# The mask product leaves the scores of two graph attentions, and VectorE adds the mask in place of ScalarE's copy

## The reference, cut to what matters

```
h = layernorm(x) @ W
e = leaky_relu(h @ a1 [:, None] + h @ a2 [None, :], 0.2)
e = where(adj > 0, e, -1e9)            # 128 x 128 for each graph
out = softmax(e) @ h
x = x + elu(out)
```

## Time and profile before

| | |
|---|---|
| median of 3 runs | 587.17 us (584.67 to 588.05) |
| the profiled execution | 585.35 us, its span 583.6 us |
| PE | 544.2 us busy, 93% of the span |
| DVE | 447.8 us, 77% |
| ACT | 418.4 us, 72% |
| POOL | 232.1 us, 40% |
| chain that ended last | PE 78%, issue 6%, DVE 5%, POOL 5%, ACT 4% |

### The profile page before, as it was taken

One profiled execution on the slowest core, in us unless ns is written; L12 is line 12 of the kernel. 1 busy time (PEld: TensorE's weight loads), 2 busy tenths in 40 slices (PEclk: granted clock), 3 DMA queues, 4 the chain that ended last, 5 costly groups with the idle time before them and its releaser, 6 DMA issues.

```text
span 583.6 us, 15065 instructions
## 1 busy us (share of the span) xinstructions
PE 544.2 (93%) x3792; PEld 452.0 (77%) x3825; DVE 447.8 (77%) x1652; ACT 418.4 (72%) x1102; POOL 232.1 (40%) x449
## 2 busy tenths in 40 slices
PE   6678999999999999999999999999977999999993
PEld 5556678777787878778777787767756799999993
DVE  3766979889898898988989888776555377777777
ACT  1355667878878788787887878877643578888883
POOL 6222214442434424334243342331322036666665
PEclk8999999999999999999999999999999799999998
DMA  8504325052250522505235051230320377777732
GB/s 202 121 14 151 95 69 165 6 160 83 82 163 1 162 79 84 159 4 162 71 91 163 0 163 35 76 110 9 102 72 2 120 223 242 247 236 218 221 119 72
DMA packets 78834, 66.46 MB, mean 114 GB/s; under 512 B 9916, under 2 KB 64460, under 8 KB 78796
## 3 DMA queue, kind: packets, MB, share of 16 engines
q1 hardware_dynamic: 65562, 60.60, 34.0%
q10 hardware_dynamic: 13234, 5.42, 3.4%
HBM read 61.57 MB, written 4.42 MB: 113 GB/s over the span
## 4 chain that ended last, share of the span: by engine, by line
PE 78%; issue 6%; DVE 5%; POOL 5%; ACT 4%; ACTq 1%; DVEq 0%; POOLq 0%
PE bank L1496 14%; PE bank L1483 13%; PE wide L206 5%; PE bank L1728 5%; PE bank L1738 4%; PE wide L1728 4%; PE wide L239 4%; PE wide L1738 4%; PE bank L1475 3%; PE bank L1476 3%; PE bank L1477 3%; PE wide L231 2%; PE wide L199 2%; PE wide L1524 2%; PE wide L220 2%
## 5 line engine op out<-in xcount | busy, mean ns | idle before, releaser
L1496 PE MATMUL bank<-w,h2w 128*128 128x128 f32 x768 | 104.2, 279 | 1.8 <-DVE h2w L1080 1.8
L1496 PEld LDWEIGHTS bank<-w,h2w 128*128 128x128 f32 x768 | 94.8, 192 | 6.9 <-DVE h2w L1080 3.0
L1483 PE MATMUL bank<-h,w 128*128 128x512 f32 x192 | 98.8, 596 | 0.3 <-ACT h L821 0.3
L816 ACT ACTIVATE h<-bank,b 128x512 f32<-128x512 f32 x96 | 66.3, 690 | 41.7 <-PE bank L1483 41.5
L821 ACT ACTIVATE h<-bank,b 128x512 f32<-128x512 f32 x96 | 66.0, 688 | 12.9 <-PE bank L1477 12.7
L1080 DVE TENSOR_TENSOR h2w<-h,wide_w 128x512 f32<-128x512 f32 x96 | 64.8, 676 | 8.2 <-ACT h L816 8.0
L1475 PE MATMUL bank<-xnTh,w1h 128*128 128x512 f32 x96 | 66.9, 697 | 0.0
L100 POOL TENSOR_TENSOR route_var_eps<-route_mean_var,eps 128x4 f32<-128x4 f32 x16 | 10.4, 651 | 115.2 <-DVE route_mean_var L93 115.1
L100 POOL TENSOR_TENSOR at_var_eps<-at_mean_var,eps 128x4 f32<-128x4 f32 x32 | 12.9, 403 | 94.0 <-DVE at_mean_var L93 94.0
L268 ACT ACTIVATE at_pr<-at_lk,at_nm 128x128 f32<-128x128 f32 x128 | 41.3, 414 | 3.6 <-DVE at_nm L303 3.6
L206 PE MATMUL wide<-at_wc,at_xT 128*128 128x130 f32 x256 | 36.0, 286 | 5.1 <-ACT at_xT L247 5.1
(11 more groups left out here) (264 smaller groups left out, 1364.0 us busy)
## 6 DMA issues: line engine op xcount, KB each, us to landing
wide_w<-w_scratch SPq DMA_DIRECT2D x96, 256.0 KB, 4.5
mask<-in_L_ffn_W SPq DMA_DIRECT2D x124, 128.0 KB, 2.4
x<-in_x SPq DMA_DIRECT2D x16, 256.0 KB, 5.1
adj_in<-in_adj SPq DMA_DIRECT2D x16, 256.0 KB, 5.8
wide_w<-bmix_scratch SPq DMA_DIRECT2D x16, 256.0 KB, 3.6
xin<-in_x SPq DMA_DIRECT2D x15, 256.0 KB, 5.6
out<-at_pr ACTq DMA_DIRECT2D x8, 256.0 KB, 3.1
out<-at_prT ACTq DMA_DIRECT2D x7, 256.0 KB, 2.8
```

Of the source, the lines that this page charges most:

```text
L816: a.activation(h2[:, e % 2, :], b_h2[:, :], ACT.Relu, bias=b2[:, e:e + 1]).then_inc(h2_ready, 1)
L1483: pe.matmul(b_h2[:, :], w2[:, e, :], h1[:, e % 2, :], start=True, stop=True).then_inc(l2_done, 1)
L1496: last = pe.matmul(b_out[:, s], h2w[:, e % 2, s], w3[:, e, :], start=False, stop=(e == E0 - 1), skip_group_check=True)
```

## The change

The product L219 is taken out in both attentions, and L220 starts the accumulation instead. `attn_act_z`, ScalarE's copy of the scores, is taken out. `attn_dve_max` begins with a new VectorE addition, which reads the scores in PSUM and the mask in SBUF and writes `lk`; the two old VectorE instructions follow it. TensorE no longer waits for the mask, VectorE waits for TensorE's scores. Nothing else moves.

```
-def attn_pe_scores(st, pe, identb, mask, spread, g):
+def attn_pe_scores(st, pe, spread, g):
     pe.wait_ge(st["rows_ready"], g + 1)
-    pe.matmul(st["bank"][:, :], identb[:, :], mask[:, cols(g)], start=True, stop=False, skip_group_check=True)
-    pe.matmul(st["bank"][:, :], st["rows"][:, :], spread[:, 0, :, :].rearrange("p t d -> p (t d)"), start=False,
+    pe.matmul(st["bank"][:, :], st["rows"][:, :], spread[:, 0, :, :].rearrange("p t d -> p (t d)"), start=True,
               stop=False, skip_group_check=True)
...
-def attn_act_z(st, a, g):
-    a.wait_ge(st["z_done"], g + 1)
-    need(a, st["x_ready"], g)
-    a.activation(st["lk"][:, :], st["bank"][:, :], ACT.Copy).then_inc(st["z_ready"], 1)
...
-def attn_dve_max(st, v, g):
+def attn_dve_max(st, v, mask, const_ready, mask_ready, g):
+
+    settle(v, const_ready)
+    v.wait_ge(st["z_done"], g + 1)
+    v.wait_ge(mask_ready, g + 1)
+    need(v, st["x_ready"], g)
+    v.tensor_tensor(st["lk"][:, :], st["bank"][:, :], mask[:, cols(g)], ALU.add).then_inc(st["z_ready"], 1)
     v.wait_ge(st["z_ready"], g + 1)
     v.scalar_tensor_tensor(st["lk"][:, :], st["lk"][:, :], SLOPE, st["lk"][:, :], ALU.mult, ALU.max)\
         .then_inc(st["lk_ready"], 1)
...
                 if attn0:
-                    attn_act_z(at0, a, i + 2)
...
-                if attn1:
-                    attn_act_z(at1, a, i - 1)
...
                 if attn0:
-                    pe.wait_ge(mask_ready, i + 3)
-                    attn_pe_scores(at0, pe, identb, mask, spread, i + 2)
+                    attn_pe_scores(at0, pe, spread, i + 2)
```

More of the change, by code:

```diff
@@ L877, in body @@
                     attn_act_elu(at1, a, i - 2)
-                if attn0:
-                    attn_act_z(at0, a, i + 2)
                 def route_relu(g):
@@ L1225, in body @@
                 if attn0:
-                    attn_dve_max(at0, v, i + 2)
+                    attn_dve_max(at0, v, mask, const_ready, mask_ready, i + 2)
                 if live("norm0", i0) and i0 != -LEAD["route"]:
@@ L1242, in body @@
                     if i0 == N:
-                        attn_dve_max(at1, v, N - 1)
+                        attn_dve_max(at1, v, mask, const_ready, mask_ready, N - 1)
                     if i0 >= N:
@@ L1267, in body @@
                 if attn1 and i0 != N:
-                    attn_dve_max(at1, v, i - 1)
+                    attn_dve_max(at1, v, mask, const_ready, mask_ready, i - 1)
                 if live("route", i0, 1) and i0 != -LEAD["route"]:
@@ L1636, in body @@
                 if attn1:
-                    attn_pe_scores(at1, pe, identb, mask, spread, i - 1)
+                    attn_pe_scores(at1, pe, spread, i - 1)
                 if run:
```

## The result

The changed kernel takes 603.69 us, the median of 6 runs (601.97 to 606.23), and the kernel before 587.49 us in 6 runs beside it (584.67 to 590.44). The ratio is 1.0278, with an interval from 1.024 to 1.0317. The forecast was 594.8 us. The direction is right and the loss is twice the forecast: 16.2 us where 7.6 were worked out.

The account below looks back on a forecast made before the run. TensorE's own stream and a mixed ring over ScalarE, VectorE and layer 3 were taken to share the bound. Losses of 3.0 + 3.0 + 1.4 + 0.7, less 0.3 and 0.2, gave +7.6 us: 594.8 us, range 586.5 to 599.

Parts of the forecast that it names:

- The ring through `at1`: L1477, ScalarE, `p_sum`, VectorE's list, layer 3, next L1477: `at1`'s addition inside it makes the next round 0.60 us late.
- The bare hand-overs: Layer 3's weight loads for e = 0 and e = 5 follow VectorE's multiplication by 0.06 us every round.
- the sum: Rounds 2 to 14 lose 3.0 + 3.0 + 1.4 us; with the last group and small savings, net +7.6 us.
- TensorE's idle time behind `h2w`: Sign: TensorE idles about 0.35 (e = 3), 0.35 (e = 5) and 0.5 (e = 0) us a round.
- it costs nothing: `at0`'s addition, ahead of L299, takes its time out of VectorE's 1.75 us wait at `p_sum`; uncovered, 0.72 a round.
- The cover: VectorE's wait at `p_sum` for ScalarE's `pe`, 1.75 us a round, taken as hiding `at0`'s addition.
- the last group: Round 16, where L299 follows a norm that waited for GpSimd and little else runs: 0.7 us lost.
- TensorE's stream deciding: Rival: TensorE's stream sets the time, so removing its products saves 7.0 us, giving 580.2 us; chance 0.12.
- The two cancelling: Rival: ScalarE's freed 0.59 brings `p_sum` forward about as much as the addition delays e = 0; 587 us, chance 0.13.
- VectorE becomes the bound: Rival: additions cost 0.93 each and nearly use up the 1.8 us cover; about +10.5 us, 597.7 us, chance 0.08.
- The rule that was weighed: Skill's rule putting each VectorE addition at 0.61 instead of 0.72, making the result 1.8 us lower; rows 4 preferred.

Follow-up runs that it names:

- e1: Kernel before with the change made in the second attention (`at1`) alone; 599.79 us, ratio 1.0229.
- e3: Changed kernel with GpSimd's subtraction for `at1` cut from 512 to 32 columns; 594.10 us, ratio 1.0116.
- e4: Changed kernel with `at0`'s addition moved ahead of the elu's first part on VectorE; 596.30 us, ratio 1.0152.
- e2: Kernel before with the change made in the first attention (`at0`) alone; 597.46 us, ratio 1.0191.
- e6: Changed kernel with `at0`'s addition made twice, the second between the first and the maximum; 613.16 us, ratio 1.0439.
- e8: Kernel before with `at0` alone changed, its addition placed early as in e4; 589.27 us, ratio 1.0024.
- e10: e8 with 37 more unread products in TensorE's idle pieces; 584.37 us, ratio 0.9963.
- e9: Kernel before with 37 more unread products in TensorE's idle pieces; 585.70 us, ratio 0.9979.
- e5: Kernel before with GpSimd's subtraction for `at1` cut from 512 to 32 columns; 586.71 us, ratio 0.9991.

## Why the forecast was half right

**The ring through `at1` holds.** 25.0 to 25.2 us a round was forecast, and e1, e3 and e4 all have 25.03 to 25.15. The bare hand-overs at e = 0 and e = 5 came. e3, which takes only GpSimd's part away, adds 7.3 us to rounds 0 to 15, where the sum had 3.0 + 3.0 + 1.4 = 7.4. That its median, 594.10, is so near the forecast 594.8 is partly luck, since e1 and e4 have the same rounds and medians of 599.79 and 596.30. TensorE's idle time behind `h2w` for e = 3, 5 and 0 is 0.33, 0.25 and 0.39 a round in e3, against the forecast 0.35, 0.35 and 0.5; in the changed kernel it is 0.06, 0.24 and 0.38.

**The step that failed** is "it costs nothing", for `at0`'s addition. The cover was there, the price was wrong. The sum left the maximum at 0.69, but moving it by 0.72 put it behind the start of GpSimd's subtraction, and it became 1.44. The text said that what is moved must be counted, and counted only VectorE's own queue. With VectorE's list written out, the five kernels below come out. In the kernel before, the list is 24.53 - (1.70 - 0.29) = 23.12 us a round, the wait at `p_sum` taken at its least. Adding what each kernel adds:

| kernel | list, worked out | round, measured | what is left for p_sum | measured |
|---|---|---|---|---|
| e1 | 23.12 + 0.72 = 23.84 | 25.09 | 1.25 + 0.29 = 1.54 | 1.5 |
| e3 | 23.12 + 1.44 = 24.56 | 25.09 | 0.82 | 0.80 |
| e4 | 23.12 + 0.72 + 0.60 = 24.44 | 25.09 | 0.94 | 0.92 |
| e2 | 23.12 + 0.72 + 0.75 + 0.57 = 25.16 | 25.09 | none | 0.29 |
| after | 23.12 + 1.44 + 0.75 + 0.59 = 25.90 | 25.79 | none | 0.29 |

The table is an account and no forecast: the 0.57 to 0.75 in it are the measured ones. Where the list is shorter than 25.09, the ring sets the round; where it is longer, the list does, to within about 0.1 us. In e2 `at1` is unchanged, so the ring has no 25.09 there, and that its list comes out at the same length is chance. The changed kernel is the only one of the five in which `at1`'s price and `at0`'s stand one on the other. The account also shows a smaller slip of the prediction: it took all of the 1.75 us at `p_sum` as cover, but the wait never falls under 0.29, so about 1.4 can be hidden. With a maximum of 0.69 that would not have mattered, since 1.44 for both additions and a round longer by 0.56 still leave 0.82.

**Of the 19.9 us by which the two profiled spans differ,** 14.65 lie in rounds 0 to 15 (378.05 - 363.40). 7.3 of them are the ring's (e3), and the other 7.4 the held maximum with what follows from it. From round 15 to the end of the pool's sums it is 2.9 us, where 0.7 was put down for the last group. e3, e1 and e4, with the same addition there, need 0.2, 1.0 and 1.2 more than the kernel before, and a 3.4 us piece at the lower clock level lies in this part of the changed kernel, so I don't count the rest for the addition. 2.6 us lie ahead of the first expert round, a part which ranged from 49.3 to 52.4 us over these kernels with no order that I can name. So the 14.65 us of the rounds explain most of the 16.2 us between the medians, and the rest stays open.

**The rivals.** TensorE's stream deciding fell, since rounds grew. The two cancelling fell as well. The third, "VectorE becomes the bound", is what happened, but with another cause: the additions cost 0.72 each, not 0.93, and the cover of 1.8 us was eaten by the maximum and by the wait at L325 that its loss brought. It was given 0.08, and its price of 10.5 us was too low also. The busy times of VectorE (30 us more instead of 22) show the same 12 x 0.75 = 9. ScalarE is 10.5 us less busy over the whole span, not the forecast 19. The 18.0 within the stretch from 60 to 420 us look nearer than they are, because fewer rounds fit into it. The forecast added up the copies' durations; the busy time counts a stretch with two overlapping instructions once, and all of ScalarE's durations added up fall by 24.5 us, so its instructions overlap less than before. Which ones I have not followed.

**The rule that was weighed,** the Trainium skill's "VectorE: DVE Perf Modes", section "The DRAIN you can't avoid", would have each addition at 0.61. From the addition to the maximum that it feeds it is 0.72 again in all kernels (269.45 to 270.17), and 0.60 where the next instruction is independent (e4). The rows decide: dependence costs 0.12 here.

## What to carry to other kernels

Before calling an inserted instruction free under a wait, look at what the instructions behind it will run beside on the other engines at their new time, GpSimd's long operations above all. A maximum moved by 0.72 us cost 0.75 more because it came second. Then write the engine's whole list as a sum for a round and set it against the ring: cover that a wait gives is spent once, and other engines may use the same wait to catch up. And where a change gains a few tenths a round, look at TensorE's granted clock outside the rounds before judging it.

## What the hardware showed that I had not expected

- **GpSimd's subtraction of 512 columns, with two SBUF inputs, and a VectorE operation with two SBUF inputs exclude each other, and the first one wins.** VectorE second: 1.44 instead of 0.69, or 1.05 instead of 0.68 for a `weigh` (e4), with the end 0.55 behind GpSimd's end. GpSimd second: 1.49 instead of 1.28. VectorE's addition from PSUM and SBUF (0.69, e6) and the one-input reduction (0.69) ran beside GpSimd undisturbed. The Trainium skill has this rule in "SBUF — State Buffer", section "SBUF: two separate sides": whichever of the two starts first has the shared pair of ports for its whole instruction and the other is blocked. The rows on this subtraction agree with it. GpSimd's roots on 4 columns don't: VectorE's multiplication with two SBUF inputs took its usual 0.68 from 0.30 behind the start of a root recorded with 1.01 (before). GpSimd's recorded spans are rough, so how long such a small operation really has the ports isn't shown. By the rule and the two start times in the kernel before (269.75 + 0.72 behind 270.09) the cost could have been forecast; the prediction didn't look there.
- **Short stretches of TensorE at 1.2 GHz come and go behind the rounds.** The kernel before had 6.8 us of it there, e8 17.1, e10 3.4 and e9 none. TensorE's busy time ahead, from 444 to 451, was 5.74, 6.09, 6.76 and 6.76 us of 7. More products in the idle pieces made the median 4.9 us shorter on e8 and 1.3 on the kernel before. Why e8 has the longer stretch with nearly the same work ahead of it as the kernel before isn't settled. e5, whose program on TensorE is that of the kernel before, has 10.2 us there, so one trace of each kernel is too little to part 6.8 from its neighbours.
